# Fetching part of the source rows by an adding gather in the second layer of a graph network

## The chip, the cores and the metric

The kernel runs on one core of one Trainium2 chip. The metric is the device time of one execution in microseconds; lower is better.

## The reference

```python
h = relu(layernorm(x));  x = x + attention_layer(h, src, dst, ...)     # first layer
h = relu(layernorm(x))
msg = concat([h[src], h[dst], edge_attr]) @ W1 + b1       # 206250 edges, 320 -> 256
x = x + segment_sum(relu(msg) @ W2 + b2, src)             # 6250 nodes, 256 -> 128
```

Edges come sorted by `dst` (6250 nodes, 206250 edges, self-loops included). In the second layer the sum runs over `src`. It is split: `h @ W1[:128] + b1` (called P here) and `h @ W1[128:256]` (Q) are computed once per node, and an edge's hidden vector is relu(P[src] + Q[dst] + edge_attr @ W1[256:]).

## The kernel before

All five engines run hand-written programs that meet at semaphores. After some preparation there are three long stages.

The attention stage (first layer) goes over 62 batches of 26 tiles of 128 edges. POOL gathers the rows of `h` by source node with one indirect DMA per tile.

The target stage (`targets`) goes over the same 1612 tiles. For each, PE computes R = Q[dst] + edge features @ W1 into PSUM, ACT copies it (line 630) into a row buffer `Rb` of 26 tiles, DVE writes a tag beside it (`tags`, line 1170: the source node's number minus 128 times its bin, a bin being 128 nodes), and POOL scatters the 257 words per edge (256 of R and the tag) into the DRAM table `xr` (line 481), at places that sort the edges by the bin of their source. `Rb` is released in four pieces when their scatters have landed. SP loads Q's rows, the targets' offsets and, for the batch after, the edge features (`load_windows`, `load_ea`). Beside it, in the first 49 batches, PE computes one bin's P per batch, and ACT and DVE split it into three bf16 parts, whose sum has fp32's precision, in `Pt` (high, middle, low).

The source stage (`sources`) goes over `xr` in 856 pairs of two tiles of 128 edges, each pair belonging to one bin. SP loads a chunk of two pairs (514 KB) into one of four slots of `XR`. Per pair:

- DVE (`hotp`, line 1259) compares a row of numbers 0 to 127 with each edge's tag: a one-hot matrix `OHp`, 128 x 128 in fp32, for each tile. POOL casts both to bf16 (`hotq`, line 495).
- PE transposes both (`turnp`, line 1583), ACT copies them out (line 687), and PE multiplies each with the bin's three parts of P (`source_rows`, line 1592: six products of 256 columns), which fetches P[src] for the 256 edges.
- DVE adds R (`add_r`, line 1267), ACT applies relu (line 693).
- PE multiplies the fp32 one-hot matrices with the hidden rows and a column of ones (`segment`, line 1602), and DVE adds the result to the bin's row of `accB` (line 1274).

The order of work is written out by hand: in turn m, PE does the transposes of pair m, the source rows of m - 1 and the segment sum of m - 3, DVE the compares of m + 1, the sum of m - 2 and the addition of m - 4, ACT the evacuation of m and the relu of m - 2. SP waits, ahead of loading chunk c, until `add_r` is done with chunk c - 4. A short end multiplies `accB` with W2 and writes the output.

Of the kernel before, what the change touches and what calls it, by code (L numbers as in the profile page):

```python
# [12 lines left out]
P = 128  # L13
# [37 lines left out]
XW = HID + 1  # L51
PM = 7
# [11 lines left out]
def gnn(nc, x, src, dst, ea, W, asrc, adst, bias, W1, b1, W2, b2, out):  # L64
# [6 lines left out]
    xr = nc.dram_tensor("xr", (XROWS + GR, XW), F32).ap()  # L71
# [4 lines left out]
    with ctx:  # L76
# [58 lines left out]
        zfill = Y([FILLR // P, XW])  # L135
# [41 lines left out]
        zlate, resd, hcol = S([2, XW]), S([HID]), S([P])  # L177
# [8 lines left out]
        Rb, EAb, EAT = S([BT, XW]), S([2, BT, DE]), S([2, P])  # L186
# [8 lines left out]
        accB, XR, OHp = S([NT, XW]), S([NS, CP, PR * XW]), S([SB, PR, P])  # L195
        OHq = S([4, PR, P], BF16)
        ohTp, hp, hid = S([2, PR, P], BF16), S([2, PR, HID]), S([2, PR, XW])
        pbrow = S([NPAIR + 16], I32, 1)
# [40 lines left out]
        def _(sp):  # L239
# [67 lines left out]
            def load_windows(b, q, first=False, more=""):  # L307
# [40 lines left out]
            load_windows(1, 1, more="next")  # L348
            with sp.Fori(1, NB // 2 - 1) as i:
# [3 lines left out]
            load_windows(NB - 1, 1)  # L353
# [32 lines left out]
        def _(pool):  # L386
# [22 lines left out]
            M.memset(zfill[:, :, HID:XW], -1.0).then_inc(sem("zf_ready"), 1)  # L409
# [32 lines left out]
            M.memset(zlate[:, :, HID:XW], -1.0).then_inc(sem("zl_ready"), 1)  # L442
# [61 lines left out]
        def _(act):  # L504
# [178 lines left out]
            def turn_outp(g, m, first):  # L683
# [3 lines left out]
                A.activation(flat(ohTp[:, m % 2, :, :]), PSB[m % 2][:].bitcast(BF16)[:, 0:PR * P], ACT.Copy).then_inc(sem("pT_ready"), 1)  # L687

            def relu(g, m, first):
# [3 lines left out]
                A.activation(hid[:, m % 2, :, 0:HID], hp[:, m % 2, :, :], ACT.Relu).then_inc(sem("hid_ready"), 1)  # L693

            def sources(i, first=False):
                for m in range(SB):
                    turn_outp(SB * i + m, m, first)
                    if not (first and m < 2):
                        relu(SB * i + m - 2, (m - 2) % SB, first)
# [3 lines left out]
            relu(NPAIR - 2, SB - 2, False)  # L703
            relu(NPAIR - 1, SB - 1, False)
# [16 lines left out]
        def _(dve):  # L721
# [68 lines left out]
            def prepare(c):  # L790
# [22 lines left out]
                elif c == 5:  # L813
                    V.tensor_copy(bin_row.rearrange("p (b t) -> p b t", t=RB)[:, :, 0:BT],
                                  ir.rearrange("p (b t) -> p b t", t=BT)).then_inc(sem("bins_ready"), 1)
# [42 lines left out]
            V.tensor_tensor(aT3[:, :, 2, :], aRes, aT3[:, :, 1, :], ALU.subtract).then_inc(sem("aT3_ready"), 1)  # L858
# [295 lines left out]
            def targets(b, q, first=False, ahead=True, part=None, prev=None):  # L1154
# [96 lines left out]
            def hotp(i, m, first):  # L1251
                s, k, g = m // CP, m % CP, SB * i + m
                if k == 0:
                    dve.wait_ge(sem(f"xr_in{s}"), 16 * (i + 1))
                if not first:
                    dve.wait_ge(sem("seg_ps"), g - SB + 1)
                for j in range(PR):
                    c = j * XW + HID
                    last = V.tensor_scalar(OHp[:, m, j, :], iota[:, 0:P], XR[:, s, k, c:c + 1], None, ALU.is_equal)  # L1259
                last.then_inc(sem("ohp_ready"), 1)  # L1260

            def add_r(g, m, first):
                s, k = m // CP, m % CP
                dve.wait_ge(sem("pp_ps"), g + 1)
                if not (first and m < 2):
                    dve.wait_ge(sem("hid_ready"), g - 1)
                V.tensor_tensor(hp[:, m % 2, :, :], PSB[2 + m % 2][:].rearrange("p (j h) -> p j h", j=PR),  # L1267
                                XR[:, s, k, :].rearrange("p (j w) -> p j w", j=PR)[:, :, 0:HID], ALU.add).then_inc(sem("hp_ready"), 1)
# [46 lines left out]
        def _(pe):  # L1315
# [89 lines left out]
            pe.wait_ge(sem("bins_ready"), 1)  # L1405
            pe.wait_ge(sem("aT3_ready"), 1)
# [179 lines left out]
            def source_rows(g, m, reg, first):  # L1586
# [3 lines left out]
                for j in range(PR):  # L1590
# [69 lines left out]
```

## Time and profile before

| | us |
|---|---|
| median of 3 runs | 5919.61 (5910.63 to 5921.62) |
| the profiled execution | 5926.82 |
| its span, first to last instruction | 5924.3 |
| attention stage, first to last gather | 146.5 to 2216.7 |
| target stage, first to last scatter | 2371.3 to 4442.2 |
| source stage, first cast to last segment sum | 4454.3 to 5860.3 |

Starts are counted from the first instruction of the span. "Idle" is an engine's time without work ahead of an instruction, followed by what ended it; "issue" means that nothing in the profile did. PE is the matrix engine, PEld its weight loads, SPq the queue of DMA issues of SP.

### The profile page before, as it was taken

To read this page: it belongs to the slowest core of one execution; us is meant where nothing else is said; L and a number is where in the kernel's file an instruction comes from. 1 tells how busy PE (TensorE), PEld (TensorE's weight loads), DVE (VectorE), ACT (ScalarE), POOL (GpSimd) and SP (SyncE) were. 2 spreads that over 40 slices of the span, in tenths; PEclk is the share of its full clock that TensorE was granted. 3 is DMA by queue.
4 is the path that set the end of the run, shared out by engine and by line. 5 is a ranking of instruction groups with operands and counts; after the bars stand their busy time and mean duration, and the time that the engine had idled before them with its cause. 6 is when DMAs were issued, how large, how long until landed. Compare 5 with 4: busy or idle time off the path is not lost.

```text
span 5924.3 us, 157615 instructions
## 1 busy us (share of the span) xinstructions
PE 5211.8 (88%) x36226; PEld 4151.3 (70%) x36227; DVE 4114.1 (69%) x13680; ACT 2689.9 (45%) x7309; POOL 3582.0 (60%) x4140
## 2 busy tenths in 40 slices
PE   3788888888888886999999999999979999999998
PEld 2577767777677774666666666666657888888887
DVE  5688878788787887555555555555538888888886
ACT  1455555555555553333233233232225555555554
POOL 0777777777777774777777777777772222222221
PEclk9689889889898887999999999999999999999999
DMA  5222222222222245998888888889875555555554
GB/s 181 63 54 54 54 54 54 53 53 53 54 53 54 53 108 151 266 263 257 258 257 252 256 251 259 253 250 266 252 210 156 162 160 160 162 162 160 160 161 124
DMA packets 786185, 927.75 MB, mean 157 GB/s; under 512 B 299696, under 2 KB 587728, under 8 KB 785814
## 3 DMA queue, kind: packets, MB, share of 16 engines
q1 hardware_dynamic: 644296, 597.68, 36.7%
q0 software_dynamic: 128960, 321.27, 18.2%
q10 hardware_dynamic: 12686, 6.51, 0.4%
q14 instruction: 205, 1.68, 0.1%
q8 instruction: 38, 0.62, 0.0%
HBM read 669.67 MB, written 255.41 MB: 156 GB/s over the span
## 4 chain that ended last, share of the span: by engine, by line
PE 51%; POOL 18%; issue 13%; DVE 10%; DVEq 4%; DMA 3%; ACT 1%; ACTq 1%; POOLq 0%; SPq 0%
POOL xr L481 17%; PE bank L1602 13%; PE bank L1443 12%; PE bank L1592 10%; PE bank L1535 4%; PE bank L1537 3%; DVE arena L971 2%; PE bank L1370 2%; DVEq L227 2%; DVE arena L864 2%; PE bank L1583 2%; DMA xr<-arena 2%; POOL arena L433 1%; PE bank L1380 1%; DVE arena L951 1%
## 5 line engine op out<-in xcount | busy, mean ns | idle before, releaser
L433 POOL DMA_INDIRECT arena<-h_tab,arena x1612 | 1578.9, 979 | 555.5 <-issue 478.9
L481 POOL DMA_INDIRECT xr<-arena x1612 | 1579.1, 980 | 519.2 <-issue 482.1
L1443 PE MATMUL bank<-arena 128*128 128x136 f32 x6448 | 1281.9, 326 | 98.7 <-DVE arena L971 9.0
L630 ACT ACTIVATE arena<-bank 128x256 f32<-128x256 f32 x1612 | 588.9, 386 | 1423.7 <-PE bank L1537 926.7
L1443 PEld LDWEIGHTS bank<-arena 128*128 128x128 f32 x6448 | 952.0, 208 | 204.1 <-issue 103.4
L1535 PE MATMUL bank<-arena 128*128 128x256 f32 x3224 | 1010.0, 395 | 22.8 <-DVE arena L1163 17.8
L549 ACT ACTIVATE arena<-bank 128x256 bf16<-128x256 bf16 x1612 | 619.9, 385 | 886.3 <-PE bank L1370 819.3
L1537 PE MATMUL bank<-arena 128*128 128x256 f32 x3224 | 975.5, 384 | 42.8 <-DVE arena L1178 39.5
L495 POOL CAST arena<-arena 128x256 bf16<-128x256 f32 x856 | 342.9, 401 | 1060.1 <-DVE arena L1259 1057.2
L1602 PE MATMUL bank<-arena 128*128 128x257 f32 x3424 | 886.0, 381 | 0.0
L971 DVE TENSOR_TENSOR arena<-arena,bank 128x272 f32 x1612 | 689.8, 428 | 185.9 <-PE bank L1443 158.6
L1537 PEld LDWEIGHTS bank<-arena 128*128 128x128 f32 x3224 | 603.8, 191 | 171.3 <-DVE arena L1178 93.8
L1592 PE MATMUL bank<-arena 128*128 x5136 | 702.6, 273 | 0.0
L556 ACT ACTIVATE arena<-arena 128x256 f32<-128x256 bf16 x1612 | 647.8, 409 | 25.2 <-PE bank L1443 21.9
L1602 PEld LDWEIGHTS bank<-arena 128*128 128x128 f32 x3424 | 586.2, 191 | 55.6 <-issue 0.3
L1535 PEld LDWEIGHTS bank<-arena 128*128 128x128 f32 x3224 | 539.2, 198 | 110.8 <-issue 32.8
L864 DVE TENSOR_SCALAR arena<-arena 128x256 bf16<-128x256 bf16 x1612 | 461.9, 290 | 207.0 <-issue 197.9
L1267 DVE TENSOR_TENSOR arena<-bank,arena 128x512 f32<-128x512 f32 x856 | 584.1, 682 | 3.1 <-PE bank L1592 2.4
L1178 DVE COPY arena<-bank 128x128 f32<-128x128 f32 x806 | 232.9, 289 | 508.8 <-PE bank L1525 508.4
L1370 PE MATMUL bank<-arena 128*128 128x128 bf16 x3224 | 483.8, 236 | 116.0 <-DVE arena L864 112.9
L693 ACT ACTIVATE arena<-arena 128x512 f32<-128x512 f32 x856 | 537.3, 628 | 100.4 <-DVE arena L1267 99.4
L687 ACT ACTIVATE arena<-bank 128x256 bf16<-128x256 bf16 x856 | 329.7, 385 | 542.3 <-PE bank L1583 542.3
(258 smaller groups left out, 6578.6 us busy)
## 6 DMA issues: line engine op xcount, KB each, us to landing
arena<-xr SPq DMA_DIRECT2D x428, 514.0 KB, 3.6
arena<-q_tab SPq DMA_DIRECT2D x1612, 128.0 KB
arena<-in_edge_attr SPq DMA_DIRECT2D x61, 832.0 KB
arena<-rel_tab SPq DMA_DIRECT2D x124, 224.0 KB
arena<-h_tab,arena POOLq DMA_INDIRECT x1612
xr<-arena POOLq DMA_INDIRECT x1612
arena<-rel_tab SPq DMA_DIRECT2D x124, 192.0 KB
xr<-arena SPq DMA_DIRECT2D x26, 514.0 KB
```

The costliest lines, as they stand in the source:

```text
L433: pool.indirect_dma_start(G[:, q, t, :], None, h_tab, bass.IndirectOffsetOnAxis(ap=idx[:, q, t:t + 1], axis=0)).then_inc(sem(f"gath{q}"), 16)
L481: pool.indirect_dma_start(xr, bass.IndirectOffsetOnAxis(ap=pos[:, q, t:t + 1], axis=0), Rb[:, t, :], None).then_inc(sem(f"scat{m}"), 16)
L549: A.activation(ohT[:, t % 2, :], PSB[t % 2][:].bitcast(BF16)[:, 0:2 * P], ACT.Copy).then_inc(sem("ohT_ready"), 1)
L556: A.activation(OH[:, (t + 2 * q) % 4, :], OHb[:, q, t, :], ACT.Copy).then_inc(sem("wide_ready"), 1)
L630: A.activation(Rb[:, t, 0:HID], PSB[(t + 2 * q) % 4][:, 0:HID], ACT.Copy).then_inc(sem("r_out"), 1)
L971: V.tensor_tensor(a, a, PSB[3 + t % 2][:, 0:2 * H * MW], ALU.add).then_inc(sem("acc_done"), 1)
L1370: last = pe.transpose(PSB[t % 2][:].bitcast(BF16)[:, k * P:(k + 1) * P], OHb[:, s, t, k * P:(k + 1) * P], identb)
L1443: last = pe.matmul(PSB[3 + t % 2][:, k * H * MW:(k + 1) * H * MW], OH[:, (t + 2 * q) % 4, k * P:(k + 1) * P], flat(msg[:, t, :, :]), start ...
L1535: pe.matmul(o, OHT[:, (t + 2 * q) % 4, :], Qw[:, t, :], start=True, stop=False)
L1537: pe.matmul(o, EAT[:, (t // 2 + q) % 2, :], w1z[:, t % 2, :], start=False, stop=True).then_inc(sem("main_done"), 1)
L1592: last = pe.matmul(PSB[2 + m % 2][:, j * HID:(j + 1) * HID], ohTp[:, m % 2, j, :], flat(Pt[:, bass.ds(reg, 1), part, :]), start=(part == 0 ...
L1602: last = pe.matmul(PSB[4 + m % 2][:, 0:XW], OHp[:, m, j, :], hid[:, m % 2, j, :], start=(j == 0), stop=(j == PR - 1))
```

## The change

The first pair of a chunk is worked on as before, apart from dtypes. In the second pair of each chunk (`k == 1`), tile 1 no longer gets its P rows from PE: POOL issues one indirect DMA per chunk that gathers the fp32 rows of P by source node from a new DRAM table `p_tab` and adds them onto R in `XR`. For that a second word, the source node's number, travels with each edge (`RW` = 258 words), DVE turns the numbers into integer indices, and ACT takes that tile's relu straight from `XR`. The table is written by SP, 128 KB per bin, during the target stage, from a copy that ACT makes.

The compares whose result is transposed (both tiles of the first pair, tile 0 of the second) are written by DVE in bf16 into `OHq`, and POOL casts them to fp32 for the segment sum. Tile 1 of the second pair is compared in fp32 and not transposed. SP's load of a chunk waits for the relu in place of the sum. In the target stage the features of the next batch are requested behind the fourth piece of windows and not behind the second.

```diff
 load_windows:
-                    if m == 1 and more:
+                    if m == 3 and part is not None:
+                        store_p(part)
+                    if m == 3 and more:
 load_xr:
-                    sp.wait_ge(sem("hp_ready"), c * CP - (NS - 1) * CP)
+                    sp.wait_ge(sem("hid_ready"), c * CP - (NS - 1) * CP)
 hotq (POOL):
-                pool.wait_ge(sem("ohp_ready"), g + 1)
-                if not (first and m < 4):
-                    pool.wait_ge(sem("pT_ps"), g - 3)
+                s, k = m // CP, m % CP
+                if k == 0:
+                    n = NS // 2 * i + s // 2
+                    pool.wait_ge(sem("idx_ready"), NB + NS * i + s + 1)
+                    pool.wait_ge(sem(f"gath{s % 2}"), GSUM + 16 * n)
+                    pool.nop(nofuse=True)
+                    pool.indirect_dma_start(XR[:, s, 1, RW:RW + HID], None, p_tab,
+                                            bass.IndirectOffsetOnAxis(ap=sidx[:, s:s + 1], axis=0),
+                                            compute_op=ALU.add).then_inc(sem(f"gath{s % 2}"), 16)
+                pool.wait_ge(sem("ohq_ready"), g + 1)
+                if not first:
+                    pool.wait_ge(sem("seg_ps"), g - SB + 1)
-                M.tensor_copy(OHq[:, m % 4, :, :], OHp[:, m, :, :]).then_inc(sem("ohq_ready"), 1)
+                M.tensor_copy(OHp[:, m, 0:PR - k, :], OHq[:, m % 4, 0:PR - k, :]).then_inc(sem("ohp_ready"), 1)
 ACT, target stage, once per part:
+                        if not (isinstance(part, int) and part == 0):
+                            act.wait_ge(sem("p_out"), 16 * part)
+                        A.activation(pout, PSB[7][:, HID:], ACT.Copy)
 turn_outp (ACT):
+                n = PR - m % CP
+                A.activation(flat(ohTp[:, m % 2, 0:n, :]), PSB[m % 2][:].bitcast(BF16)[:, 0:n * P], ACT.Copy)...
 relu (ACT):
+                if k == 0:
+                    A.activation(hid[:, m % 2, :, 0:HID], hp[:, m % 2, :, :], ACT.Relu).then_inc(sem("hid_ready"), 1)
+                else:
+                    A.activation(hid[:, m % 2, 0, 0:HID], hp[:, m % 2, 0, :], ACT.Relu)
+                    act.wait_ge(sem(f"gath{s % 2}"), GSUM + 16 * (c + 1))
+                    A.activation(hid[:, m % 2, 1, 0:HID], XR[:, s, 1, RW:RW + HID], ACT.Relu).then_inc(sem("hid_ready"), 1)
 tags (DVE, target stage):
+                    V.tensor_copy(Rb[:, lo:hi, HID + 1], srcE[:, bass.ds(B + lo, hi - lo)])
 hotp (DVE):
                 if k == 0:
                     dve.wait_ge(sem(f"xr_in{s}"), 16 * (i + 1))
+                    V.tensor_scalar(sidx[:, s:s + 1], XR[:, s, 1, RW + HID + 1:RW + HID + 2], 0.0, None, ALU.max).then_inc(sem("idx_ready"), 1)
+                if not (first and m < 4):
+                    dve.wait_ge(sem("pT_ps"), g - 3)
+                    dve.wait_ge(sem("ohp_ready"), g - 3)
 ...
-                    last = V.tensor_scalar(OHp[:, m, j, :], iota[:, 0:P], XR[:, s, k, c:c + 1], None, ALU.is_equal)
+                    o = OHp[:, m, j, :] if k and j else OHq[:, m % 4, j, :]
+                    last = V.tensor_scalar(o, iota[:, 0:P] if k and j else iotab[:, 0:P], XR[:, s, k, c:c + 1], None, ALU.is_equal)
 add_r (DVE): the same sum over n = PR - k tiles in place of PR
 turnp, source_rows (PE):
-                for j in range(PR):
+                for j in range(PR - m % CP):
```

## Rows read from the trace of the kernel before

**Rows 1.** Table of stretches: busy us of PE, PEld, DVE, ACT, POOL; PEclk; DMA share; GB/s
```profile
900.00:2000.00 1100.00, 913.09 (x7630) 781.51 (x7630) 883.55 (x3388) 625.24 (x1941) 839.16 (x857) 0.89 0.24 53
2600.00:3500.00 900.00, 850.28 (x4807) 604.26 (x4806) 470.69 (x1600) 277.66 (x815) 686.46 (x701) 1.00 0.88 257
5000.00:5700.00 700.00, 700.00 (x5129) 589.48 (x5128) 593.14 (x1708) 399.73 (x855) 171.03 (x427) 1.00 0.56 161
```

**Rows 2.** Target stage: line 481 alone, ACT's longest DMA wait, line 630's group
```profile
L481 POOL DMA_INDIRECT xr<-arena x1612: 956/962/2373, 2371.3 to 4442.2; - x180
its engine sat idle before it (us, times) until:
  issue: 482.1, 1578
...
ACT arena L630 <- DMA xr<-arena: 487.7, 163, 5.8
...
L630 ACT ACTIVATE arena<-bank 128x256 f32<-128x256 f32 x1568 | 572.3, 386 | 1386.4 <-PE bank L1537 896.4 <-DMA xr<-arena 487.7 <-issue 1.2
```

**Rows 3.** Chain that ended last, and groups by shape, from 4800 to 5600 us
```profile
by line: PE bank L1602 53.2%; PE bank L1592 40.0%; PE bank L1583 6.8%
...
L1267 DVE TENSOR_TENSOR arena<-bank,arena 128x512 f32<-128x512 f32 x489 | 333.6, 682 | 0.0
...
L1259 DVE TENSOR_SCALAR arena<-arena 128x128 f32<-128x128 f32 x978 | 232.6, 280 | 64.7 <-PE bank L1602 64.7
L1274 DVE TENSOR_TENSOR arena<-arena,bank 128x257 f32 x489 | 204.7, 419 | 56.6 <-PE bank L1602 55.3
L495 POOL CAST arena<-arena 128x256 bf16<-128x256 f32 x488 | 195.5, 401 | 603.8 <-DVE arena L1259 603.8
```

**Rows 4.** Timeline of the source stage: start us, us, engine, line, operation
```profile
5103.94 0.27 PE L1583 MATMUL bank<-arena 128*128 128x128 bf16 x2
...
5104.05 0.82 PE L1592 MATMUL bank<-arena 128*128 x6
...
5104.60 0.47 DVE L1259 TENSOR_SCALAR arena<-arena 128x128 f32<-128x128 f32 x2
5104.71 1.03 PE L1602 MATMUL bank<-arena 128*128 128x257 f32 x4
5104.99 0.68 DVE L1267 TENSOR_TENSOR arena<-bank,arena 128x512 f32<-128x512 f32 x1
...
5105.58 0.27 PE L1583 MATMUL bank<-arena 128*128 128x128 bf16 x2
...
5105.85 0.37 SPq L362 DMA_DIRECT2D arena<-xr  x1
...
5106.17 0.62 ACT L693 ACTIVATE arena<-arena 128x512 f32<-128x512 f32 x1
```

**Rows 5.** Timeline of the change from target to source stage
```profile
4442.20 0.96 POOL L481 DMA_INDIRECT xr<-arena  x1 [0.31 <-issue]
4445.52 2.17 SPq L362 DMA_DIRECT2D arena<-xr  x4
```

**Rows 6.** Line 433 alone; groups by shape of the attention and the target stage
```profile
L433 POOL DMA_INDIRECT arena<-h_tab,arena x1612: 940/947/1809, 146.5 to 2216.7; - x180
...
L864 DVE TENSOR_SCALAR arena<-arena 128x256 bf16<-128x256 bf16 x1600 | 458.0, 290 | 207.0 <-issue 197.9 <-ACT arena L556 7.3
...
L844 DVE TENSOR_SCALAR arena<-arena 128x1638 bf16<-128x1638 bf16 x59 | 37.2, 631 | 0.0
...
L1170 DVE SCALAR_TENSOR_TENSOR arena<-arena 128x6 f32 x116 | 20.2, 175 | 67.0 <-DMA xr<-arena 66.7
```

**Rows 7.** DMA queues, source and target stage, and landing time of `xr` loads
```profile
q1 hardware_dynamic: 66421, 128.55, 55.8%
...
q0 software_dynamic: 67396, 184.84, 28.7%
...
DMA to landing us min/median/max: 3.5/3.7/3.9
```

More of the change, by code:

```diff
@@ L51 @@
 XW = HID + 1
+RW = HID + 2
+GSUM = 16 * BT * (NB // 2)
 PM = 7
@@ L70, in gnn @@
     rel_tab = nc.dram_tensor("rel_tab", (T * P,), BF16).ap()
-    xr = nc.dram_tensor("xr", (XROWS + GR, XW), F32).ap()
+    xr = nc.dram_tensor("xr", (XROWS + GR, RW), F32).ap()
+    p_tab = nc.dram_tensor("p_tab", (NPAD, HID), F32).ap()
     pb_tab = nc.dram_tensor("pb_tab", (P * PBJ,), I32).ap()
@@ L134, in gnn @@
         thruF, thruB, contN = Y([TP], BF16, 1), Y([TP], BF16, 1), Y([TP], F32, 1)
-        zfill = Y([FILLR // P, XW])
+        zfill = Y([FILLR // P, RW])
         Z0 = Y.at
@@ L176, in gnn @@
         S = Region(X0 + PW, Y0)
-        zlate, resd, hcol = S([2, XW]), S([HID]), S([P])
+        zlate, resd, hcol = S([2, RW]), S([HID]), S([P])
+        pout = Region(X0 + PW)([HID])
         S = Region(X0, X0 + PW - NT * P)
@@ L185, in gnn @@
         S = Region(Y0, WORDS - NB * RB)
-        Rb, EAb, EAT = S([BT, XW]), S([2, BT, DE]), S([2, P])
+        Rb, EAb, EAT = S([BT, RW]), S([2, BT, DE]), S([2, P])
         OHT, oh49 = S([4, P]), S([2, BT, NT], BF16)
@@ L194, in gnn @@
         S = Region(Y0)
-        accB, XR, OHp = S([NT, XW]), S([NS, CP, PR * XW]), S([SB, PR, P])
+        accB, XR, OHp = S([NT, XW]), S([NS, CP, PR * RW]), S([SB, PR, P])
         OHq = S([4, PR, P], BF16)
         ohTp, hp, hid = S([2, PR, P], BF16), S([2, PR, HID]), S([2, PR, XW])
-        pbrow = S([NPAIR + 16], I32, 1)
+        pbrow, sidx = S([NPAIR + 16], I32, 1), S([NS], I32)
         S = Region(X0, Y0)
@@ L305, in load_ea_last, with store_p, load_windows @@
                 sp.dma_start(EAb[0:ELAST, 1, BT - 1, :], ea[r0 + (BT - 1) * P:E, :]).then_inc(sem("ea_last"), 16)
-            def load_windows(b, q, first=False, more=""):
+            def store_p(n):
+                sp.wait_ge(sem("hi_ready"), NCH * NQ + n + 1)
+                sp.dma_start(p_tab[bass.ds(n * P, P), :], pout).then_inc(sem("p_out"), 16)
+            def load_windows(b, q, first=False, more="", part=None):
                 B = b * BT
@@ L347, in _ @@
             sp.wait_ge(sem("x1_out1"), 16 * (NCH // 2))
-            load_windows(1, 1, more="next")
-            with sp.Fori(1, NB // 2 - 1) as i:
+            load_windows(1, 1, more="next", part=0)
+            with sp.Fori(1, NT // 2) as i:
+                for q in range(2):
+                    load_windows(2 * i + q, q, more="next", part=2 * i + q - 1)
+            store_p(NT - 2)
+            with sp.Fori(NT // 2, NB // 2 - 1) as i:
                 for q in range(2):
@@ L352, in _ @@
             load_windows(NB - 2, 0, more="last")
-            load_windows(NB - 1, 1)
+            load_windows(NB - 1, 1, part=NT - 1)
             sp.wait_ge(sem("main_done"), T)
@@ L408, in _ @@
             pool.wait_ge(sem("zf_ready"), 1)
-            M.memset(zfill[:, :, HID:XW], -1.0).then_inc(sem("zf_ready"), 1)
+            M.memset(zfill[:, :, HID:RW], -1.0).then_inc(sem("zf_ready"), 1)
             M.memset(aT[:, NT, :], 0.0).then_inc(sem("aT0"), 1)
@@ L441, in _ @@
             pool.wait_ge(sem("zl_ready"), 1)
-            M.memset(zlate[:, :, HID:XW], -1.0).then_inc(sem("zl_ready"), 1)
+            M.memset(zlate[:, :, HID:RW], -1.0).then_inc(sem("zl_ready"), 1)
             pool.wait_ge(sem("cols_used"), 2)
@@ L686, in turn_outp, with relu @@
                     act.wait_ge(sem("pp_ps"), g - 1)
-                A.activation(flat(ohTp[:, m % 2, :, :]), PSB[m % 2][:].bitcast(BF16)[:, 0:PR * P], ACT.Copy).then_inc(sem("pT_ready"), 1)
-            def relu(g, m, first):
+                n = PR - m % CP
+                A.activation(flat(ohTp[:, m % 2, 0:n, :]), PSB[m % 2][:].bitcast(BF16)[:, 0:n * P], ACT.Copy).then_inc(sem("pT_ready"), 1)
+            def relu(g, m, c, first):
+                s, k = m // CP, m % CP
                 act.wait_ge(sem("hp_ready"), g + 1)
@@ L698, in sources @@
                     if not (first and m < 2):
-                        relu(SB * i + m - 2, (m - 2) % SB, first)
+                        relu(SB * i + m - 2, (m - 2) % SB, NS // 2 * i + (m - 2) // (2 * CP), first)
             sources(0, True)
@@ L702, in _ @@
                 sources(i)
-            relu(NPAIR - 2, SB - 2, False)
-            relu(NPAIR - 1, SB - 1, False)
+            relu(NPAIR - 2, SB - 2, NS // 2 * NTURN - 1, False)
+            relu(NPAIR - 1, SB - 1, NS // 2 * NTURN - 1, False)
             for c in range(NCH):
@@ L1257, in hotp @@
                 for j in range(PR):
-                    c = j * XW + HID
-                    last = V.tensor_scalar(OHp[:, m, j, :], iota[:, 0:P], XR[:, s, k, c:c + 1], None, ALU.is_equal)
-                last.then_inc(sem("ohp_ready"), 1)
+                    c = j * RW + HID
+                    o = OHp[:, m, j, :] if k and j else OHq[:, m % 4, j, :]
+                    last = V.tensor_scalar(o, iota[:, 0:P] if k and j else iotab[:, 0:P], XR[:, s, k, c:c + 1], None, ALU.is_equal)
+                last.then_inc(sem("ohq_ready"), 1)
             def add_r(g, m, first):
@@ L1266, in add_r @@
                     dve.wait_ge(sem("hid_ready"), g - 1)
-                V.tensor_tensor(hp[:, m % 2, :, :], PSB[2 + m % 2][:].rearrange("p (j h) -> p j h", j=PR),
-                                XR[:, s, k, :].rearrange("p (j w) -> p j w", j=PR)[:, :, 0:HID], ALU.add).then_inc(sem("hp_ready"), 1)
+                n = PR - k
+                V.tensor_tensor(hp[:, m % 2, 0:n, :], PSB[2 + m % 2][:].rearrange("p (j h) -> p j h", j=PR)[:, 0:n, :],
+                                XR[:, s, k, :].rearrange("p (j w) -> p j w", j=PR)[:, 0:n, 0:HID], ALU.add).then_inc(sem("hp_ready"), 1)
             def add_up(g, m, reg):
@@ L1589, in source_rows @@
                     pe.wait_ge(sem("hp_ready"), g - 1)
-                for j in range(PR):
+                for j in range(PR - m % CP):
                     for part in range(3):
```

9 lines of the change are left out of this document (4 added, 5 removed).

## Prediction

> **What bounds the kernel now.** I read the table of stretches first, to find the stage that the change touches [rows 1]. There are three long stages. In the attention stage POOL issues 1612 gathers, in the target stage 1612 scatters, and in the source stage (from 4.45 ms on) POOL does only casts. The target stage is POOL's: the scatters' 0.96 us and the 0.30 us between two make 1.26 us, and from the first to the last scatter 2071 us pass for 1612, or 1.285 us each [rows 2]; ACT and DVE wait there for scatters that have landed [rows 2]. A little work more on ACT, DVE or SP is hidden there.
>
> In the source stage PE has no idle time at all [rows 1], and the chain that ended last names there PE's three lines and nothing else worth a per cent [rows 3]. The timeline gives PE's period [rows 4]. A pair's transposes start at 5103.94, the source rows' products at 5104.05, the segment sum's at 5104.71, the next pair's transposes at 5105.58. So 0.11 + 0.66 + 0.87 = 1.64 us per pair, times 856 pairs 1404 us, which is the length of the stage. One transpose is 0.055 us, one source-row product 0.11 us. The other engines have room: of 700 us DVE is busy for 593, ACT for 400, POOL for 171 [rows 1], which is 1.39, 0.94 and 0.40 us per pair.
>
> **The change part by part.** *PE.* In 428 of 856 pairs one of two tiles loses its transpose and its three source-row products: 0.055 + 3 x 0.11 = 0.385; I take 0.38, since the starts are rounded. 428 x 0.38 = 163 us. A chunk (two pairs) goes from 3.28 to 2.90 us. All of this lies on the path that sets the end, as long as no other engine or transfer needs more than 2.90 us per chunk. The rest of the working asks that.
>
> *DVE.* Three of four compares per chunk become bf16 to bf16. The bf16 compare of 256 elements takes 290 ns, one of 1638 takes 631 ns [rows 6]: 0.25 ns per element, so 128 should take 258 ns against 280 now [rows 3]; bounds 258 and 280. The sum with the rows read is half as long in one pair: 256 elements at 1.03 ns (682 - 419 ns over 512 - 257, [rows 3]), 0.26 us less. The index conversion is new: 0.17 us by the six-element DVE operation [rows 6]. Two more waits per pair that no row prices: from nothing to 0.04 us each, a tenth of the distance from one step's start to the next [rows 4]. Per chunk 2.78 - 0.07 - 0.26 + 0.17 = 2.62, with the waits 2.78 us. Both are under 2.90, so it costs nothing; DVE is then the busiest engine after PE.
>
> *ACT.* In one pair the 512-element relu (0.62 us, [rows 4]) becomes two of 256 (0.39 us for such an operation, [rows 2]), and one evacuation halves: at most 1.88 + 0.16 = 2.0 us per chunk. Hidden. But the second half waits for the gather, and behind it stand the next pair's evacuation and relu, for which PE waits.
>
> *POOL.* Casts go the other way and one of two is half as long: 0.40 us [rows 3] and 0.20 to 0.40 us. They are no longer between compare and transpose, only before the segment sum, two periods later. The gather is new: 1.26 us by gathers and scatters alike [rows 2, 6]. With 0.1 us of waiting ahead of each: 1.3 + 0.4 + 0.3 + 0.1 = 2.1 us of 2.90. The trace has no accumulating gather. Lower bound 1.26 us; upper bound two instructions' worth, 2.5 us, if each row needs a second descriptor. I take 1.3, as plain gather and plain scatter differ by 0.015 us.
>
> *Is the gather back in time?* The last scatter starts at 4442.20, and the first instructions that wait for it run at 4445.5, 3.3 us later [rows 5]. The index is there with the first compare of the chunk, some six PE periods (8.7 us) before PE wants the second pair's relu; less 0.65 us (compare after the period's start) and 0.4 us (relu) 7.6 us are left. Cast in progress 0.4 + 0.3 + 3.3 = 4.0 us, with twice the movement 4.4 us. Hidden, by 3 us.
>
> *DMA engines.* The chunk loads keep the 16 engines busy for 0.558 of the time [rows 7], 1.83 us per chunk; 258 words per row for 257 add 0.4%. 1402 scatters of 128 x 1028 bytes took 28.7% of 1800 us, 0.37 us each [rows 7]. The adding gather moves as much and also reads its destination: bounds 0.37 and 1.1 us (three movements); I take 0.75. Sum 2.6 us of 2.90 at my value: 0.89, which is what the target stage holds [rows 1].
>
> *The ring of chunks.* Four slots; SP's load now waits for the relu, not for the sum. Before: the sum starts at 5104.99, the load is issued at 5105.85, lands 3.7 us later at 5109.55 [rows 4, 5, 7], and the compare that needs it would come at 5104.60 + 4 x 1.64 = 5111.15: 1.6 us to spare. After: the relu of the same pair ends at 5106.79 [rows 4], in two halves some 0.15 us later, so the issue is 1.2 us later, and four periods are 0.75 us shorter. The load is 0.35 us late for the compare's natural place, more with the gather beside it. That place has slack (compare to transposes about 2 us). The limit is the loop: chunk there, its compares and PE's next transposes (2.1 us), evacuation, relu (1.4), issue (0.1), landing D, and this three chunks later: 3.6 + D <= 8.7, so D may be 5.1 us. It is 3.7 now; with 0.4 to 1.1 us of gather in its way 4.1 to 4.8. It holds, by 0.3 to 1.0 us. This is the thinnest cover of the change; each us of D above 5.1 costs 0.33 us per chunk, 143 us in all.
>
> *Elsewhere.* 49 ACT copies of 256 (0.38 us each) and 49 stores of 128 KB in the target stage, four small DVE copies per batch (0.17 us), the features' load behind the last windows: all lie where ACT, DVE and PE wait for scatters [rows 2], and the features are wanted a whole batch (33 us) later. Uncovered, the copies would be 19 us and the tags 42 us. The first gather of the stage adds at most its 4 us where PE's first pairs hide none of it; I take 2.
>
> *Sum.* Profiled execution 5926.8 us (span 5924.3 and 2.5 around it) - 163 + 2 = 5766. The median of the runs is 7 us lower than the profiled one: 5759, say **5760 us**.
>
> **A rule against it.** With the attention stage's bf16 compares running beside them, gathers take 0.947 us in the median, scatters beside the target stage's compares 0.962 [rows 2, 6]: no sign of POOL held up by DVE's fast compares. The Trainium skill, "SBUF — State Buffer", in its part on port contention, says that DVE's two-port modes, which such compares can enter, and GpSimd exclude each other for a whole instruction, descriptor writing included. By that rule POOL could lose each compare's time, which is the third rival below.
>
> **The rivals.** *Ring or gather late (0.20).* For it: the 0.3 to 1.0 us of cover. Against: the loads' landings are tight, 3.5 to 3.9 us. At D = 6 us the chunk takes 3.2 us: 428 x 0.3 = 128 us of the gain are gone, 5888. The case spans 5795 to 5908. *Adding gather heavy on the DMA engines (0.12), the one that ends slower.* From 1.07 us of engine time per gather it shows (2.90 - 1.83), from 1.45 us, four times a plain scatter's, the kernel is slower than before. At five times, 1.85 us, the chunk takes 3.68: 428 x 0.40 = 171 us slower, 6091. Against: a copy with one more read is not four copies. *POOL held up (0.05).* If each of four compares (0.27 us) blocks POOL: 2.1 + 1.1 = 3.2 us per chunk, 5888; with doubled descriptors 1.3 us more, 4.5 and slower, which I count in the 0.12. *Nothing gained (0.03):* the chunk settles at 3.28 us, 5920. The forecast has 0.60.
>
> **How the numbers follow.** 0.2%, 12 us, is what a measurement of this kernel tells from no change. The likeliest case has its own range, 5745 to 5795 (at best 0.41 us per chunk are saved, at worst each chunk loses 0.08 us). Both late cases and POOL's reach 5908; up to 5885 they hold about half of their 0.25. With the slower case, nothing gained and their tails some 0.2 left out, the range is 5742 to 5885. Faster 0.83, same 0.04, slower 0.13.
>
> **What would show it.** Right: source stage about 1240 us, PE without idle, 5136 source-row matmuls become 3852, the chain still PE's. DVE 0.85 to 0.9 busy, POOL 0.6 to 0.75, chunk loads landing in 4 to 5 us. POOL's gather near 0.95 us. Target stage still 1.285 us per scatter. Wrong by the ring: DVE's compares idle for a DMA of the row table, once per chunk. Wrong by the gather: ACT's second relu idle for a DMA of the new table. Wrong by POOL: the gather's duration above 1.5 us. Most dangerous to the number are the landing time of loads beside adding gathers and their engine time, neither of which the trace has.

## The result and the profile after

The changed kernel takes 5840.5 us (median of 3 runs, 5839.25 to 5850.25) against 5919.61: a ratio of 0.9868 [0.9854, 0.9882], 79 us less. The forecast's likeliest case was 5760, 159 us less. Half of the gain is missing. The profiled execution took 5850.25 us, 84 more than the 5766 of the sum.

All of that is in the source stage. The target stage is as it was: its scatters run from 2370.6 to 4436.9 us, 2066 us for 1612 as against 2071 [rows 2]. The source stage, from its first transposes to its last segment sum, by the two lines of PE that open and close it (duration min/median/max in ns, then first and last start):

```profile
L1623 PE MATMUL bank<-arena x1284: 217/218/314, 4448.4 to 5776.5; 128*128 128x128 bf16 x184
L1642 PE MATMUL bank<-arena x3424: 377/381/479, 4453.1 to 5781.2; 128*128 128x257 f32 x191
```

5781.2 - 4448.4 = 1332.8 us. By the same lines the kernel before has 5860.6 - 4454.8 = 1405.8. The forecast, 856 x 1.64 - 163, was 1241, so 92 us are missing in the stage. Below, "the stage" is always this stretch, and a turn is 8 pairs, or 4 chunks. 107 turns make the stage: 12.46 us per turn, where PE's own work would take 4 x 2.90 = 11.6.

The stretch of the source stage that answers to [rows 1] (for each engine busy us and instructions, then clock, DMA share, GB/s):

```profile
5000.00:5700.00 700.00, 688.73 (x4512) 541.24 (x4511) 587.55 (x2030) 428.65 (x1128) 500.30 (x678) 1.00 0.91 212
```

PE looks nearly as full as before, 688.73 of 700 us, and that is the trap of this case: a busy share cannot tell that the same work lasts longer. The chain of waits can. One turn of it (start us, us, what):

```profile
5105.54 0.87 PE bank L1642 x4
5106.41 0.08 issue
5106.48 0.28 PE bank L1623 x2
5106.77 0.48 PE bank L1632 x3
5107.24 1.09 PE bank L1642 x4
5108.34 0.06 PE bank L1623
5108.40 0.66 PE bank L1632 x6
5109.05 0.88 PE bank L1642 x4
5109.93 0.11 PE bank L1623 x2
5110.04 0.33 PE bank L1632 x3
5110.36 0.87 PE bank L1642 x4
...
5117.73 0.87 PE bank L1642 x4
5118.60 0.23 issue
5118.83 0.28 PE bank L1623 x2
```

From 5108.34 to 5111.23 a chunk takes the 2.89 us of the forecast, and so do those that follow. At 5106.48 and 5118.83, 12.35 us apart, something else happens: 0.08 to 0.23 us pass in which nothing is issued, and then the transposes take 0.28 instead of 0.11 us, the products 0.48 instead of 0.33, the segment sum 1.09 instead of 0.87. So PE starves for a moment and then fills again. From one of these restarts to the next that costs about 0.77 us: 0.17 + 0.15 + 0.22 in the slow start and 0.23 ahead of the next. It is not the clock: the granted clock is 1.00 here as in [rows 1].

What PE's own queue does there is told by the register load, with which each turn reads 12 bins. First the kernel before, then the kernel after:

```profile
L233 PEldq TENSOR_LOAD <-arena x108: 844/848/858, 4453.5 to 5855.6; - x108
```
```profile
L237 PEldq TENSOR_LOAD <-arena x108: 846/1142/1303, 4447.5 to 5776.7; - x108
L237 DVEq TENSOR_LOAD <-arena x108: 846/851/1170, 4447.8 to 5776.8; - x108
L237 PEldq TENSOR_LOAD <-arena x1: 1161/1161/1161, 5105.2 to 5105.2; - x1
```

The load that starts at 5105.2 takes 1.16 us and ends at 5106.36. The array, with the segment sum that started at 5105.37, is done at about 5106.4, and the next transposes, which are issued behind the load, come at 5106.48 and slowly. In before the corresponding load starts at 5109.0, takes 0.85 us, and the array is busy 0.6 us beyond its end.

The remaining rows from 4800 to 5600 us (waits, then groups, then DMA):

```profile
POOL arena L511 <- DVE arena L1299: 116.8, 122, 2.2
POOL arena L511 <- DMA arena<-p_tab,arena: 66.7, 54, 1.6
DVE arena L1290 <- DMA arena<-xr: 52.0, 107, 1.3
ACT arena L727 <- DMA arena<-p_tab,arena: 0.4, 1, 0.4
```
```profile
L511 POOL DMA_INDIRECT arena<-p_tab,arena x258 | 405.6, 1572 | 228.4 <-DVE arena L1299 116.8 <-DMA arena<-p_tab,arena 66.7 <-PE bank L1642 26.9
L518 POOL CAST arena<-arena 128x256 f32<-128x256 bf16 (+1 forms) x516 | 314.8, 869 | 0.3 <-DVE arena L1299 0.3
L1290 DVE TENSOR_SCALAR arena<-arena 128x1 int32<-128x1 f32 x258 | 38.3, 149 | 54.1 <-DMA arena<-xr 52.0
```
```profile
q0 software_dynamic: 37152, 33.83, 27.2%
arena<-xr SPq DMA_DIRECT2D x258, 516.0 KB, 4.0
```

ACT waits for a gather once, 0.4 us: they are not late. DVE waits for chunk loads 107 times in 258 chunks, and these land after 4.0 us in the median. The gathers hold the DMA engines for 27.2% of 800 us over 258 chunks, 0.84 us each. Two suspects are left, PE's register load and the ring of chunks.

### The profile page after: what moved, and what is told of

It reads as the page before. It is cut to its first block, busy times and chain, and to the rows that moved or that the text cites. A ratio compares the mean times of both kernels' runs of the same rounds, so it can differ in the third digit from the quotient of the medians.

```text
span 5848.5 us, 158779 instructions
## 1 busy us (share of the span) xinstructions
PE 5110.8 (87%) x34514; PEld 3993.4 (68%) x34515; DVE 4058.5 (69%) x14356; ACT 2722.8 (47%) x7786; POOL 4173.7 (71%) x4568
## 4 chain that ended last, share of the span: by engine, by line
PE 49%; POOL 16%; issue 14%; DVE 10%; DMA 5%; DVEq 4%; ACT 1%; ACTq 1%; POOLq 0%; SPq 0%
POOL xr L495 15%; PE bank L1483 14%; PE bank L1642 11%; PE bank L1632 7%; PE bank L1575 4%; PE bank L1577 4%; PE bank L1411 3%; DMA xr<-arena 3%; DVEq L231 2%; DVE arena L1005 2%; DVE arena L898 2%; POOL arena L447 2%; PE bank L1623 1%; PE bank L1421 1%; DMA arena<-xr 1%
## 5 line engine op out<-in xcount | busy, mean ns | idle before, releaser
L573 ACT ACTIVATE arena<-bank 128x256 bf16<-128x256 bf16 x1612 | 618.3, 384 | 891.1 <-PE bank L1411 849.3
L511 POOL DMA_INDIRECT arena<-p_tab,arena x428 | 673.0, 1572 | 382.0 <-DVE arena L1299 197.8
L1642 PE MATMUL bank<-arena 128*128 128x257 f32 x3424 | 899.1, 385 | 1.4 <-ACT arena L727 0.8
L1632 PE MATMUL bank<-arena 128*128 x3852 | 568.8, 274 | 7.0 <-DVE arena L1308 6.1
L1197 DVE TENSOR_SCALAR arena<-arena 128x128 f32<-128x128 bf16 x1612 | 470.3, 302 | 82.2 <-PE bank L1577 44.8
L518 POOL CAST arena<-arena 128x256 f32<-128x256 bf16 x856 | 522.4, 871 | 0.3 <-DVE arena L1299 0.3
L1299 DVE TENSOR_SCALAR arena<-arena 128x128 bf16<-128x128 bf16 (+1 forms) x1712 | 429.2, 300 | 111.7 <-PE bank L1623 59.2
```

The lines of the kernel that those rows point to most:

```text
L511: pool.indirect_dma_start(XR[:, s, 1, RW:RW + HID], None, p_tab, bass.IndirectOffsetOnAxis(ap=sidx[:, s:s + 1], axis=0), compute_op=ALU.ad ...
L573: A.activation(ohT[:, t % 2, :], PSB[t % 2][:].bitcast(BF16)[:, 0:2 * P], ACT.Copy).then_inc(sem("ohT_ready"), 1)
L1632: last = pe.matmul(PSB[2 + m % 2][:, j * HID:(j + 1) * HID], ohTp[:, m % 2, j, :], flat(Pt[:, bass.ds(reg, 1), part, :]), start=(part == 0 ...
L1642: last = pe.matmul(PSB[4 + m % 2][:, 0:XW], OHp[:, m, j, :], hid[:, m % 2, j, :], start=(j == 0), stop=(j == PR - 1))
```

## The experiments

Ratios are to the kernel before on the same chip in the same call. e1 to e4 ran on one chip, m1 and n1 on another, on which the kernel before takes 8228 us; the surplus is all ahead of the source stage, which e4, a copy of before, has as long as elsewhere (1404 us). Ratios from there hold some 50 to 60 us that the stages ahead of it gain there (e2: 127 us in all, 70 in the stage), so these runs are compared by the length of the stage. Diffs are to the kernel after unless said otherwise.

### Another place for PE's register load (e1, e2)

```
 def sources(i, first=False):
+    if not first: segment(SB * i - 4, 4, False)    # e2: here; e1: behind the load
     regs = pair_bins(ENG.PE, i)
     for m in range(SB):
         ...
-        if not (first and m < 3):
+        if m < SB - 1 and not (first and m < 3):
             segment(...)
```

e1 issues a turn's last segment sum behind the register load, e2 ahead of it as before and only turns the loop by one sum.

> The changed kernel with PE's register load of the pairs' bins (once per turn of 8 pairs) moved from the turn's start to just ahead of the last segment sum of the turn before, where PE's sequencer waits for the relu anyway. Theory A (the missing 80 us is this load, no longer covered: 0.77 us in each of 107 turns): the regular step from turn to turn disappears, source stage about 1245 us, about 5760 us. Theory B (the ring: chunk loads land too late for DVE's compares, 0.2 us per chunk, and PE's gap at the turn is a coincidence of eight pairs and four slots): unchanged within 10 us of 5840.

> The changed kernel with the same rotation of PE's loop, so that the loop's branch comes ahead of that segment sum, but the register load stays in its old place, between segment sum and transposes. Theory A: unchanged, about 5840, since the load is what costs. Variant A2 (branch and instruction fetch at the loop's end cost, not the load): about 5760. Theory B: 5840.

e1: 0.9874 [0.9857, 0.989], stage 1356.8 us, 24 longer than after. e2: 0.9843 [0.9826, 0.9859], stage 1333.9, as after. My first theory, that the load costs less further ahead, fell. In e1's chain of waits both suspects show, one after the other:

```profile
7205.31 0.31 issue
7205.63 1.13 PE bank L1642 x4
...
7211.53 0.41 ACT arena L727
7211.96 0.05 SPq L376
7212.11 3.83 DMA arena<-xr
7215.96 0.07 DVE arena L1290
...
7216.84 0.34 DVE arena L1308
...
7217.52 0.41 ACT arena L727
7217.95 0.05 SPq L376
```

PE restarts with a segment sum of 1.13 us. Later the chain leaves PE altogether: relu, SP's load, 3.83 us of landing, the index of the landed chunk, behind it on DVE the addition of R (L1308) for an earlier pair, that pair's relu, and SP's next load. From load to load 5.99 us, and by the order of DVE's instructions (worked out below) that is a lap of two chunks, for which PE needs 5.8.

### The load twice (e3, e4, i1, i2)

e3 (after) and e4 (before) read the bins a second time into registers that nobody uses.

> The changed kernel with a second register load per turn on PE, its values unused, behind the segment sum of the fourth pair (the same place of a chunk as the turn's end). Theory A: the gap of 0.77 us appears twice per turn, up to 80 us slower: 5900 to 5920. Theory B: PE waits for the ring anyway, so at most 10 us slower.

> The kernel before with the same second load. Theory A: hidden as the first is, since the load is over 0.6 us ahead of the next transposes: 5920, no change within 6 us. Rival (each load costs PE something even here, which the trace doesn't show): 5990 to 6000.

0.9852 [0.9835, 0.9868] and 1.0001 [0.9985, 1.0017]. But each trace has 108 register loads as before: the compiler had left the unused ones out. These runs repeat after and before (stages 1329.8 and 1404.3 us) and say nothing on the load. i1 (before) and i2 (after) do it with registers that are used:

```
 for m in range(SB):
+    if m == 4:
+        regs = pair_bins(ENG.PE, i)      # and the same on DVE
```

> The kernel before with the same second loads, used. PE's load ends there 0.6 us ahead of the next transposes, and DVE has 0.2 us of idle per pair: hidden, within 8 us of 5920. If each load always costs something: 5960 or more.

> The changed kernel in which PE and DVE load their bins a second time in each turn, ahead of the fifth pair, and use the values (the second loads of the two earlier runs were unused and left out by the compiler, as their loads' count shows). Theory L (a register load is on the path at each turn, PE's about 0.4 + 0.4 us and DVE's 0.85 to 1.0 us): 60 to 100 us slower than the changed kernel, 5900 to 5945. Rival (the ring alone sets 12.4 us per turn and loads fall into its slack): within 15 us of 5840.

i1: 0.9998 [0.9988, 1.0008], stage 1404.6: no cost at all in before. i2: 0.9862 [0.9846, 0.9879], stage 1323.8, 9 less than after. So a second load is not a second stall. The added one, in mid-turn, is hidden nearly whole even in after; it starts 0.7 us ahead of its segment sum, the turn's own, behind the loop's branch, only 0.2. What counts is how much is queued for the array when the load begins.

### The ring of chunks (g1, g2, g3)

g1 has six slots instead of four, with turns of 12 pairs, a one-hot ring of six and 864 pairs for 856; each turn reads 16 bins. g2 adds a second, unused load. g3 is g1 with its loads issued only three chunks ahead:

```
-NS = 4
+NS = 6                                    # g1; SB follows: 12 pairs
...
-                    sp.wait_ge(sem("hid_ready"), c * CP - (NS - 1) * CP)
+                    sp.wait_ge(sem("hid_ready"), c * CP - 3 * CP)      # g3
```

> The changed kernel with six chunk slots in place of four. A turn of the loops becomes 12 pairs, so the register loads of PE and DVE come once per 12 pairs, and the pairs are padded to 864 from 856 (fp32 one-hot matrices in a ring of six to make room). Theory R (ring of chunks: load of a slot waits for its relu, 4 us to land, 7.9 us from compare to relu, 12.1 to 12.4 us per turn of four slots): no more limit, source stage 432 x 2.90 = 1253 us and some 5, about 80 us shorter than the changed kernel's 1330 us in its profile. Theory L (register loads once per turn cost 0.77 us each): 72 loads in place of 107, 1253 + 55 = 1308 us. If neither, 432 x 3.10 = 1340 us.

> As the six slots, with one more register load on PE and on DVE in the middle of each turn (values unused), so there is one per 6 pairs. Theory R: source stage still 1253 to 1265 us, the loads are covered by the longer ring. Theory L: 143 loads of 0.77 us, 1253 + 110 = 1363 us.

> As the six slots, but SP loads a chunk only when the relu of the fourth chunk before it is done, so no more than four are ever in use: the old ring with the longer turn. Theory R: limit back, 432 x 3.0 to 3.1 = 1300 to 1340 us. Theory L: as with six slots, 1308 us or less; if the ring costs nothing 1253 us.

g1: 0.9868 [0.9852, 0.9885], stage 1319.8 us for 432 chunks, 3.055 per chunk against after's 3.114. g2's unused load was left out too, so it is a second g1 (0.9868 [0.9852, 0.9885], 1315.6). g3: 0.9933 [0.9917, 0.995], stage 1359.5, 40 us longer with the same code. PE's register loads grow with it, from 1.19 to 1.32 us in the median, which is 9 us at most; the rest is the depth of the ring. DVE's wait for chunks, gone in g1, is back in g3:

```profile
DVE arena L1294 <- DMA arena<-xr: 76.4, 133, 2.7
```

What g1 still loses sits at the turn, as in after, where the load of 16 bins takes 1.19 us. And per turn it loses no less than after (the table below), although DVE no longer waits for chunks: its 13 us come from having 72 turns in place of 107. A short ring can cost time, as g3 shows; that it costs any in after is not shown by these runs.

### PE early, DVE late (h3, h4)

h4 has four slots, h3 g1's six. PE's load stands ahead of the last segment sum as in e1; DVE's goes behind its first sum:

```
-    regs = pair_bins(ENG.DVE, i)
     for m in range(SB):
         ...
+        if m == 0:
+            regs = pair_bins(ENG.DVE, i)
```

> Six slots, with both register loads moved: PE's ahead of the last segment sum of the turn before, DVE's behind the first compare and sum of the turn, ahead of its addition to the bin's row. Theory T (two limits of nearly the same height, ring of four 12.1 to 12.4 us per turn and uncovered loads 11.6 + 0.8): with both gone PE sets the pace, 432 x 2.90 + 5 = 1258 us for the source stage, 5775 to 5785 us in all. If POOL (2.75 us per chunk at its fastest) or DVE now limits: 1290 us or more.

> The same two moves with the four slots of the changed kernel. Theory T: the ring's limit stays, 12.1 us per turn, source stage 1295 to 1330 us, 5805 to 5840 us in all. If loads alone were the loss: 1240 to 1250 us, 5760 us.

h3: 0.9891 [0.9875, 0.9908], stage 1347.6, 28 longer than g1. h4: 0.9898 [0.9881, 0.9914], stage 1349.6. Both lose. h3 shows how, with a load of 1.35 us from 5112.2 on:

```profile
5113.89 0.92 PE L1646 MATMUL bank<-arena 128*128 128x257 f32 x3 [1.17 <-ACT arena L729]
```

The array idles 1.17 us. The releaser named, ACT, is not it; the load, which leaves no semaphore, is. Ahead of the sum only bf16 products of 0.11 us are queued, while behind it four fp32 matmuls of 0.22 us cover 0.87 us. The early place is the place with the least cover.

### A plain gather, and a loop without branches (e6, k6)

e6 lets the gather overwrite instead of add, so R is left out of one tile in four:

```
 bass.IndirectOffsetOnAxis(ap=sidx[:, s:s + 1], axis=0),
-compute_op=ALU.add).then_inc(...)
+).then_inc(...)
```

> The changed kernel with the gather of the new table not adding: it overwrites R with P for one tile in four, so R is left out of those rows. Theory R: POOL's 1.56 us instruction falls to the 0.96 us of a plain one and the DMA engines' share falls from 0.91 to 0.80 or less; chunk loads land in 3.8 for 4.0 us, so the source stage loses 20 us at most, 1310 us. Rival P (POOL, gather and casts, sets the pace at the turn): all of the missing 80 us come back, 1250 us.

0.9823 [0.9806, 0.9839], stage 1301.2, 32 less than after. The gather shrinks, and, which I had not thought of, so does PE's register load:

```profile
L511 POOL DMA_INDIRECT arena<-p_tab,arena x266 | 257.1, 967 | 326.9 <-DVE arena L1298 220.0 <-PE bank L1641 104.2 <-issue 2.8
L517 POOL CAST arena<-arena 128x256 f32<-128x256 bf16 (+1 forms) x532 | 173.1, 348 | 44.3 <-DVE arena L1298 42.8
L237 PEldq TENSOR_LOAD <-arena x108: 845/850/867, 4449.0 to 5746.8; - x108
```

At the turn its chain has no "issue" left, but still slow transposes and products:

```profile
5115.06 0.28 PE bank L1622 x2
5115.33 0.52 PE bank L1631 x3
5115.86 1.07 PE bank L1641 x4
```

k6 writes PE's loop out fourfold, so that three of four turns have no branch; the loads stay.

> The changed kernel with PE's loop over turns unrolled four times (the loads stay, one per turn; the branch comes in 26 turns of 106). Theory S: turns without a branch have their load hidden, as the load in the middle of the turn was: 80 of 107 turns gain up to 0.77 us, 5780 to 5800. Rival R: the stall goes elsewhere in the turn, 5810 to 5840.

0.9859 [0.9843, 0.9875], stage 1329.2, 4 us from after and 1 from its repeat e3. In time the branch is worth nothing, but turn by turn the trace shows that it matters. In the 80 turns without a branch PE's load starts 0.49 us ahead of the segment sum in the mean, and the transposes behind it come 0.03 us late; in 25 with one it is 0.09 and 0.34 us. What is won there is lost again one pair later: PE then waits 0.29 us, not 0.11, for DVE's addition of R.

### The dose of the load (k1, n1, k5, k3)

k1 reads 8 bins per turn instead of 12; for PE they begin three places on:

```
-        def pair_bins(engine, i):
+        def pair_bins(engine, i, off=0):
-                pbrow[0:1, bass.ds(i * SB, SB + 4)], ...
+                pbrow[0:1, bass.ds(i * SB + off, SB)], ...
-                regs = pair_bins(ENG.PE, i)
+                regs = pair_bins(ENG.PE, i, 3)
```

> The changed kernel with 8 bins in each register load in place of 12 (only those that are used). 12 values take 0.85 us on DVE and 16 took 1.10, so 8 take 0.6 us, and PE's load some 0.3 us more beside an adding gather, 0.9 for 1.14 us. Theory S (PE's sequencer: load and branch together last longer than the segment sum's products that are queued ahead): PE's gap at the turn, 0.2 us and as much again while the queue fills, closes in part or wholly: 25 to 80 us faster than the changed kernel, 5760 to 5815. Rival R (ring of four, 12.1 to 12.4 us per turn): no more than 30 us, 5810 or more.

I expected a shorter load. For DVE it did (0.6 us), but PE's became more than twice as long as DVE's:

```profile
L237 PEldq TENSOR_LOAD <-arena x108: 1931/1938/2364, 4441.5 to 5849.3; - x108
L237 DVEq TENSOR_LOAD <-arena x108: 594/598/861, 4441.8 to 5848.9; - x108
```

The time: 5920.81, 0.9996 [0.9987, 1.0006], the whole gain gone, stage 1411.2. The load is 0.80 us longer than after's, 107 x 0.80 = 86 us, and the stage is 78 us longer: nine tenths of what the load grows by is lost. This miss became the best evidence there is. n1 gives the same slow load to the kernel before:

> The kernel before with PE's load of k1: 8 bins from the odd place, 1.94 us in place of 0.85. Its load starts about 0.6 us ahead of the array's segment sum, which lasts 0.87 us: cover of 1.5 us. Theory S: 0.45 us uncovered and up to 0.5 us of refill per turn, 50 to 100 us slower than the kernel before, 5970 to 6020. If PE's sequencer is further ahead than that: 5920.

1.0111 [1.009, 1.0132], stage 1504.3 for 1405, and at the turn of its chain there is now what before never had:

```profile
7207.80 0.48 issue
7208.27 0.28 PE bank L1583 x2
7208.56 0.94 PE bank L1592 x6
```

0.48 us uncovered, then 0.17 + 0.28 us of filling: 0.93 us for a load 1.09 us longer, times 107 the stage's 99 us. k5 is k1 with PE's and DVE's loops written out fourfold, k3 the same with six slots and 12 bins from an odd place:

> Both: 8 bins per load, PE's and DVE's loops unrolled four times, four slots. Theory S without R: source stage 1245 us, 5760. With R behind it: 107 turns of 12.1 us, 1295 us, 5805.

> The same with six slots (864 pairs). Neither the turn nor the ring is left: PE's 432 x 2.90 = 1253 us and 5 for the start, 5775. If it is no better than the four slots, POOL or DVE limits: 5800 or more.

k5: 0.9964 [0.9951, 0.9976], stage 1394.1. k3: 1.0128 [1.0111, 1.0145], stage 1478.3, with loads of 3.24 us in the median (2.87 to 3.70).

Both were meant to lose nothing at the turn. What rules them is the long load, and with it the place at which PE's bins begin.

### Two short loads in place of one (m1)

m1 reads four bins ahead of pair 0 and four ahead of pair 4 of each turn, PE from a row of its own, shifted so that its four begin at a multiple of four:

```
 for m in range(SB):
+    if m % 4 == 0:
+        regs = pair_bins(ENG.PE, i, m)    # 4 bins; PE: pbpe, DVE: pbrow
...
-                        source_rows(..., regs[m + 3], first)
+                        source_rows(..., regs[m % 4], first)
```

> The changed kernel with each register load split: 4 bins at the turn and 4 ahead of the fifth pair, on PE and on DVE, PE's from a row of its own in which they begin at a multiple of four. 12 and 16 values took 0.85 and 1.10 us, so 4 take 0.35 us, beside adding gathers 0.65 in place of 1.14. Theory S (length of PE's load at the turn): 0.5 us less per turn or more, the gap of 0.2 us and the refill behind it close: 107 x 0.5 to 0.77 us, 5760 to 5790. Rival R (ring of four chunks is the next limit at 12.1 us per turn): 5805. If neither: 5840.

0.9795 [0.9777, 0.9813]; after's repeats on the other chip of this kind, e2 and e3, had 0.9843 and 0.9852. Stage 1297.9 us, the shortest of all, 35 less than after, 12.13 per turn. DVE still waits for chunk loads, 53.7 us in the 800 from 7000 on.

```profile
L238 PEldq TENSOR_LOAD <-arena x215: 331/517/809, 6720.1 to 8014.8; - x108
```

## Why the prediction was wrong

**PE's term was right.** 3852 source-row matmuls as forecast, and 2.89 us for a chunk away from the turn where 2.90 was said.

**The step that failed: "All of this lies on the path that sets the end, as long as no other engine or transfer needs more than 2.90 us per chunk. The rest of the working asks that."** It asked DVE, ACT, POOL, the DMA engines and the ring. It did not ask PE's own sequencer. In before PE's register load hides under the 0.6 us that the queue is ahead and the 0.87 us of a segment sum, with about 0.6 us to spare. After, the turn's load starts less than 0.2 us ahead of that sum, and it takes 1.14 us. The cover is gone.

The table shows it by turns, with the stage divided by 107 (by 72 for g1 and g3, whose turns have 12 pairs). A step is the time from the start of one pair's transposes to the start of the next pair's. Undisturbed, steps of 1.31 and 1.58 us alternate (2.89 per chunk; 1.64 each in before and n1). The last four columns give what a turn's steps take beyond that in the mean: the last step, at whose end the load stands, the first and the second step behind the load, and all others together.

| kernel | PE's load, us (median) | us per turn | last step | first | second | others |
|---|---|---|---|---|---|---|
| before | 0.85 | 13.1 | 0 | 0 | 0 | 0 |
| n1, before with the slow load | 1.94 | 14.06 | 0.63 | 0.30 | 0 | 0 |
| m1 | 0.61 at the turn, 0.46 in mid-turn | 12.13 | 0 | 0.28 | 0.15 | 0.11 |
| e6 | 0.85 | 12.16 | 0.08 | 0.36 | 0.07 | 0.07 |
| after | 1.14 | 12.46 | 0.28 | 0.40 | 0.19 | 0.01 |
| k6 | 1.19 | 12.42 | 0.10 | 0.36 | 0.34 | 0.04 |
| k1 | 1.94 | 13.19 | 1.18 | 0.38 | 0.03 | 0.01 |
| g1, 12 pairs | 1.19 | 18.33 | 0.32 | 0.38 | 0.20 | 0.05 |
| g3, 12 pairs | 1.32 | 18.88 | 0.51 | 0.42 | 0.39 | 0.17 |

All of the loss in after lies in the three steps about the load. The last step is too long where the load outlasts what is queued. The first is too long because PE's queue has little or nothing in it by then: in after the three products at 5106.7 us start 0.12 us apart, each as it is issued, and not 0.11. How much is left in the queue when the load ends is the lead plus 0.87 us less the load: 0.60 us in before, where nothing is lost, 0.31 in m1, 0.10 in e6, and 0.14 too little in after, 0.49 in n1, 0.97 in k1. m1 and e6 show that the queue need not run dry for the first step to suffer.

**The second step: "3.6 + D <= 8.7, so D may be 5.1 us ... It holds, by 0.3 to 1.0 us."** D came out at 4.0 us, just under the 4.1 to 4.8 forecast, and yet DVE waits for a chunk 107 times in 258, 52 us in 800. The step followed the wrong lap: the landed chunk through its own compares, transposes and relu. The tighter one runs through DVE's order. There the index and the compares of chunk c stand directly ahead of the addition of R for the second pair of chunk c - 2, and the relu behind that addition is what frees the slot for chunk c + 2. So a wait for chunk c holds up the load of chunk c + 2. The timeline of after:

```profile
5104.37 0.15 DVE L1290 TENSOR_SCALAR arena<-arena 128x1 int32<-128x1 f32 x1 [0.17 <-DMA arena<-xr]
...
5105.19 0.41 DVE L1308 TENSOR_TENSOR arena<-bank,arena 128x256 f32<-128x256 f32 x1
...
5105.95 0.40 ACT L727 ACTIVATE arena<-arena 128x256 f32<-128x256 f32 x1
...
5110.57 0.15 DVE L1290 TENSOR_SCALAR arena<-arena 128x1 int32<-128x1 f32 x1
```

Index to the end of the relu 1.98 us here (1.6 to 2.0 in four laps), 0.18 to the issue of the load, 4.0 to land: 5.8 to 6.2 us for two chunks, and 6.20 pass between the two indices. PE's work takes 5.8. In this form the condition is 1.6 to 2.0 + 0.18 + D <= 5.8, so D may be 3.6 to 4.0 us and not 5.1. In before the slot was freed by that addition, one relu earlier, and the lap had 4 x 1.64 = 6.56 us. That the lap can be on the path is shown by e1's chain and by g3 against g1 (40 us). In after its waits cost nothing that the runs show.

**How the 92 us divide.** By the table 0.28 x 107 = 30 us are lost in the last step, 0.40 x 107 = 43 in the first and 0.19 x 107 = 20 in the second, 93 in all. The first 73 are PE's register load: n1 makes both losses in the kernel before, where there were none. Loads of 0.85 us or less bring back 32 (e6) to 35 us (m1) of the 92; each run changes something else too, e6 the gather and m1 DVE's load, but the two agree. The 20 us of the second step are DVE's: in 42 of 104 turns PE's products come late there, and in each of them they start 0.15 to 0.16 us after the end of that addition of R, by DVE, which frees their place in PSUM. In the turn at 4958 us DVE comes late with its compares because a register load of its own, 0.85 us, stands ahead of them; h3 and h4 moved that one only together with PE's, so what it costs alone stays open. The ring has no share that the runs show. g1, in which DVE waits for no chunk, loses 0.95 us per turn and after 0.88; the 13 us between them are 35 turns fewer (some 32 us), four chunks more (12 us) and a load of 16 values for 12. In m1 the 0.15 and 0.11 us of the second and the other steps may be the ring's. Whether it limits a kernel with short loads would be told by six slots with short, aligned loads, which were not tried.

**The rivals.** The forecast had given "ring or gather late" 5795 to 5908, in which the result lies. That is luck: the sign that it named for the ring, DVE idle for the row table, is there, but the time went by a cause that no rival named. "Adding gather heavy on the DMA engines" did not come: 0.84 us each where I took 0.75. "POOL held up" did not come either: beside the same bf16 compares e6's plain gathers take 0.967 us, near the 0.962 and 0.947 of [rows 2, 6]. Its sign, a gather above 1.5 us, came true for another reason: the gather adds. The Trainium skill, "SBUF — State Buffer", section "SBUF: two separate sides", says that a DVE operation in a two-port mode and a GpSimd operation shut each other out for a whole instruction; no run here shows a gather made longer by it.

**Terms of the wrong size that cost nothing.** The adding gather takes POOL 1.56 us, not 0.95. Gather and casts come to 2.8 us per chunk as recorded (405.6 + 314.8 us over 258) for a forecast of 2.1 with all gaps; the records overlap, and POOL is busy 500 of 700 us, or 2.2 per chunk. It still waits for DVE and DMA. DVE's 587.55 us in 700 are 2.6 us per chunk; forecast 2.62 to 2.78, although a bf16 compare takes 0.30 us and not 0.26. Target stage, copies and tags: no cost, as said. In 800 us POOL waits 66.7 us for its own gathers, and nobody waits for POOL.

## What to carry to other kernels

When a change shortens the engine that bounds a kernel, ask that engine's own instruction stream as well: register loads and branches that lay under its queue's lead come to light when the work above them shrinks, and a busy share near 100% hides it, while the chain's durations of the same instruction show it. Count where in the loop the lost time sits before dividing it among suspects; DVE's waits for the ring looked like a cause and were not one here. Read a ring by what is queued behind the wait for its data: if that work frees another slot, the lap is only the chunks between the two. Put a register load where the longest work is queued for the array and no branch stands ahead of it, keep it small, and let its values begin at a multiple of four, as all the quick ones here did.

## What the runs showed of the hardware that was not expected

- A register load costs by its values: 4 take 0.34 us, 8 take 0.60, 12 take 0.85, 16 take 1.10, about 0.063 us each beyond 0.09. These all begin at a multiple of four. On PE 8 values that begin three places on took 1.93 us, and 12 such 2.87 or more; other offsets were not tried. The Trainium skill, "DMA: Bandwidth & Descriptors", section "Latency and other measured facts", gives such a load a floor of about 600 ns; the 4-value loads of m1 undercut it, and the measurement decides.
- Beside adding gathers PE's register loads last longer, in the median 0.95 to 1.19 us for the 0.85 of 12 values, and POOL's casts too (0.87 us for 0.35 in the mean, both forms). Beside plain gathers neither does. Why is open.
- An adding gather of 128 rows takes POOL 1.57 us and a plain one 0.97; the DMA engines spend 0.84 us on the one and 0.60 us on the other (19.9% of 800 us for 266 in e6).
- The loop's branch on PE took 0.4 us of the lead that PE's queue had over the array (k6: 0.09 us with it, 0.49 without).
- Loads into registers that nothing reads are not in the compiled program: to double such a cost, the second copy must be used.
